# Attention and expert layer on one core: side products spread anew between the score blocks, and more masks laid by ScalarE

## What is computed

```python
# attention: 16 heads of 16; heads 0-3 see all earlier tokens, heads 4-15 a window of 64
qkv = xn @ w_qkv + b_qkv
w   = softmax(where(mask, -inf, q @ k.T * 16 ** -0.5))
att = concat_heads(w @ v) @ w_out + b_out
# experts: two branches (forward and inverse) of 8 experts of rank 64
prod    = (Q @ V) * cumsum(K @ W, axis=time)
weights = softmax(gelu(Q @ router_w1.T + b1) @ router_w2.T + b2 + bias)
branch  = (einsum(prod * weights, U) + weights @ b) / position
ffn     = (branch_fwd + alpha * branch_inv) @ W_O.T
```

## Time and profile before

| what | value |
|---|---|
| median of 3 runs | 1491.48 us (1486.11 to 1492.9) |
| the profiled execution | 1491.34 us, span 1489.6 us |
| busy TensorE, VectorE, ScalarE, GpSimd | 93%, 66%, 52%, 39% of the span |
| mean granted TensorE clock | 0.989 of full speed |
| DMA queue of SyncE | 150.59 MB, 38.8% of 16 engines' span |

### The profile page before, as it was taken

How to read it: one execution, slowest core, us unless ns; L and a number is a source line. 1 busy time by engine, 2 the same in 40 slices (tenths; PEclk the granted TensorE clock), 3 DMA queues, 4 the chain that set the end, 5 groups by cost and what they waited for, 6 DMA issues and landing times.

```text
span 1489.6 us, 35980 instructions
## 1 busy us (share of the span) xinstructions
PE 1379.5 (93%) x14481; PEld 1035.7 (70%) x14481; DVE 989.5 (66%) x2082; ACT 776.1 (52%) x1368; POOL 586.5 (39%) x663
## 2 busy tenths in 40 slices
PE   5978999999999999999999999999999999999996
PEld 4567685777758677586856778587775868667773
DVE  6667777567756777557875677566875578656661
ACT  2434537455464735645374554646356453755544
POOL 1025343453514444253433525144452534335341
PEclk9999999999999999999999999999999999999998
DMA  8430625326062541616353171624516153431610
GB/s 189 102 94 11 168 79 127 105 65 174 25 175 70 121 126 49 166 32 151 96 123 107 40 196 30 158 87 107 141 42 163 44 146 100 118 109 42 172 40 15
DMA packets 166614, 152.88 MB, mean 103 GB/s; under 512 B 37809, under 2 KB 149808, under 8 KB 166448
## 3 DMA queue, kind: packets, MB, share of 16 engines
q1 hardware_dynamic: 166448, 150.59, 38.8%
HBM read 108.57 MB, written 35.65 MB: 97 GB/s over the span
## 4 chain that ended last, share of the span: by engine, by line
PE 62%; DVE 15%; ACT 8%; issue 6%; DMA 4%; POOL 2%; SPq 1%; ACTq 0%; POOLq 0%; DVEq 0%
PE PS L676 30%; PE PS L787 11%; PE PS L821 4%; DVE rest L1193 3%; PE PS L880 3%; ACT HE L1063 3%; PE PS L807 3%; PE PS L909 3%; PE PS L898 2%; PE PS L963 2%; DMA weights_d<-weights_t 2%; DVE area L1198 2%; DVE area L1196 2%; ACT HE L1055 2%; ACT PS L1048 1%
## 5 line engine op out<-in xcount | busy, mean ns | idle before, releaser
L1504 POOL TENSOR_TENSOR PL<-prod,PH 128x512 fp32r<-128x512 f32 x128 | 164.7, 1287 | 201.3 <-ACT PH L1037 201.3
L676 PE MATMUL PS<-XH,WH 128*128 128x512 f32 x512 | 218.6, 427 | 21.7 <-ACT prod L1027 10.3
L1037 ACT ACTIVATE PH<-prod 128x512 fp32r<-128x512 f32 x128 | 80.8, 632 | 268.8 <-DVE prod L1305 252.8
L1499 POOL TENSOR_TENSOR prod<-prod,rest 128x512 f32<-128x512 f32 x96 | 124.8, 1303 | 242.9 <-DMA rest<-weights_d 166.6
L1229 DVE TENSOR_REDUCE block_peak<-PS 128x4 f32<-128x512 f32 x288 | 179.8, 685 | 48.0 <-PE PS L821 47.9
L676 PE MATMUL PS<-XH,WL 128*128 128x512 f32 x512 | 204.1, 399 | 0.0
L676 PE MATMUL PS<-XL,WH 128*128 128x512 f32 x512 | 203.6, 398 | 0.0
L1482 POOL TENSOR_SCALAR_AFFINE_SELECT HE<-HE 128x256 f32<-128x256 f32 x128 | 51.2, 406 | 364.2 <-ACT HE L1063 360.6
L1063 ACT ACTIVATE HE<-PS 128x512 f32<-128x512 f32 (+1 forms) x320 | 159.9, 553 | 33.5 <-PE PS L880 30.5
L1305 DVE TENSOR_TENSOR prod<-PS,prod 128x512 f32<-128x512 f32 x128 | 87.8, 686 | 97.3 <-PE PS L676 84.5
L676 PEld LDWEIGHTS PS<-XH,WH 128*128 128x128 f32 x512 | 97.1, 190 | 63.2 <-ACT prod L1027 16.8
(11 more groups left out here) (186 smaller groups left out, 3064.6 us busy)
## 6 DMA issues: line engine op xcount, KB each, us to landing
parts_d<-area SPq DMA_DIRECT2D x32, 768.0 KB, 5.0
area<-parts_d SPq DMA_DIRECT2D x128, 192.0 KB, 7.9
rest<-weights_d SPq DMA_DIRECT2D x192, 128.0 KB, 3.0
area<-parts_d SPq DMA_DIRECT2D x32, 576.0 KB, 7.8
tok<-in_L_attn_x_dram SPq DMA_DIRECT2D x16, 512.0 KB, 6.2
xt<-in_L_attn_x_dram SPq DMA_DIRECT2D x16, 512.0 KB, 4.1
wide<-weights_d SPq DMA_DIRECT2D x64, 128.0 KB, 3.0
out_dram<-xt SPq DMA_DIRECT2D x16, 512.0 KB, 3.8
```

Of the source, the lines that this page charges most:

```text
L676: ins = e.matmul(ps, a, b, start=first and k == 0, stop=last and k == n - 1, skip_group_check=True)
L1037: e.activation(PH[:, h, :], prod[:, j % 3, :], ACT.Copy).then_inc(phi)
L1499: e.tensor_tensor(prod[:, j % 3, :], prod[:, j % 3, :], wide[j % WIDE], ALU.mult).then_inc(weighed)
L1504: e.tensor_tensor(PL[:, j % 2, :], prod[:, j % 3, :], PH[:, j % 2, :].bitcast(F32), ALU.subtract).then_inc(plo)
```

## The change

1. The first three lpeak masks of each chunk but the first, and that of lscore (1, 0, 1), are laid by ScalarE. The three lpeak masks stand in the global stage, before its last gav; the fourth lpeak, on bank 4, keeps TensorE's mask. The peaks' banks start anew at bank 5 in each chunk.
2. x(1) and x(2) of the next chunk move from behind the global stage into it; values(1) moves from there to behind the last gav, and values(0), now on bank 7, to just before the last gav. vshift and the global stacks follow values(1). gate_parts stands one group earlier, finish(ch, 0) in the middle. weigh(0), (1) and (2) stand together behind chigh.
3. The last two groups of the expert stage, c(7) with product(7) and mix(6), stand behind all peaks.
4. In the local stage both turns stand behind the first unit; mix(7), both sums and the rows behind the second; and one parts block behind each of the others.
5. The last gscore tile is computed in all its 256 columns a head rather than 128; what is read of it is as before.
6. In the first chunk norm(1) runs in one piece behind the first four peaks, x(1) comes before it and x(2) after it. In the last chunk finish(15, 0) stands in the middle of the global stage instead of behind its first score pair.

```diff
--- before.py
+++ after.py
@@ -180,7 +180,7 @@
             add("parts_out", ch, w)
 
     def add_values(ch, u):
-        add_on("values", ch, u, uses=["bank2" if ch else f"bank{2 + u}"])
+        add_on("values", ch, u, uses=[("bank7", "bank2")[u] if ch else f"bank{2 + u}"])
         if u == T // 2 - 1:
             add("vshift", ch)
 
@@ -243,7 +243,7 @@
                 order[-1].append((add_seed, scores[2 * n + 3][4], "lscore", *scores[2 * n + 3][:4]))
             if n:
                 order[-1].append((add_lav, ch, *units[n - 1]))
-        return order
+        return order, [(add_seed, scores[1][4], "lscore", *scores[1][:4])]
 
     def global_groups(ch):
         order = []
@@ -258,7 +258,7 @@
 
         order = []
         for j in range(2 * KB):
-            if j < 2 * KB - 1 and (j > 1 or not ch):
+            if 1 < j < 2 * KB - 1:
                 order.append([(add_x, ch, j + 1, part) for part in range(2)] + [(add_weigh, ch, j + 1)])
             order.append([(add_c, ch, j, part) for part in range(2)] if j else [])
             order[-1].append((add_product, ch, j))
@@ -308,11 +308,12 @@
 
     def peak_groups(ch):
         c = ch % NC
+        turns["peak"] = 0
         order = [[(add_lpeak, ch, t, grp, peak_use())] for t in range(T) for grp in range(NL // 4)]
         gpeaks = [[(add_gpeak, ch, t, j, peak_use())] for t in range(T) for j in range(c * T + t + 1)]
         masks = [[] for _ in order + gpeaks]
         for n, ((stage, *key),) in enumerate(order + gpeaks):
-            if stage is add_lpeak and n >= PEAKS:
+            if stage is add_lpeak and (n >= PEAKS or ch and n < PEAKS - 1):
                 masks[n].append((add_seed, key[-1], "lpeak", *key[:-1]))
             elif stage is add_gpeak and key[2] == c * T + key[1]:
                 masks[n].append((add_seed, key[-1], "gpeak", *key[:-1]))
@@ -320,11 +321,9 @@
         gpeaks[2].append((add_rows, ch, 0))
         gpeaks[-1].append((add, "found", ch, 1))
         order += gpeaks
-        if ch == 0:
-            add_norm(1, order)
         blocks = range(0, len(order), PEAKS)
         joined = lambda groups, n: [stage for group in groups[n:n + PEAKS] for stage in group]
-        return [joined(order, n) + joined(masks, n + PEAKS) for n in blocks]
+        return [joined(order, n) + joined(masks, n + PEAKS) for n in blocks], joined(masks, 0)
 
 
     add("boot")
@@ -379,30 +378,44 @@
     add_weigh(0, 0)
     for part in range(2):
         add_c(0, 0, part)
+    for part in range(2):
+        add_x(0, 1, part)
+    add_weigh(0, 1)
 
     for ch in range(CHUNKS):
         nxt = ch + 1 < CHUNKS
 
-        experts, peaks = expert_groups(ch), peak_groups(ch)
+        experts = expert_groups(ch)
+        peaks = next_peaks if ch else peak_groups(ch)[0]
         split = len(experts) - (0 if nxt else 4)
         if ch:
             experts[1].append((add_finish, ch - 1, 1))
-            experts[2], experts[3] = experts[3], experts[2]
-        run(experts[0] + peaks[0])
-        weave(experts[1:split], peaks[1:])
+        experts[2], experts[3] = experts[3], experts[2]
+        if ch:
+            run(experts[0] + peaks[0])
+        else:
+            run(peaks[0])
+            for n in range(len(NORM)):
+                add("norm", 1, n)
+            run([(add_x, 0, 2, part) for part in range(2)] + [(add_weigh, 0, 2)] + experts[0])
+        weave(experts[1:split - 2], peaks[1:])
+        locals_, first_mask = local_groups(ch)
+        for group in [first_mask] + experts[split - 2:split]:
+            run(group)
         if ch:
             add_residual(ch)
 
         last_mix = [(add_mix, ch, 2 * KB - 1, part) for part in range(2)]
         if nxt:
-            side = [[(add_turn, ch + 1, 0)], last_mix, [(add_turn, ch + 1, 1)], [(add, "sums", ch + 1, 0), (add_rows, ch, 1)]]
-            side += [[(add_parts, ch + 1, 1, 0), (add, "sums", ch + 1, 1)]]
-            side += [[(add_parts, ch + 1, w, b)] for w, b in ((1, 1), (0, 0), (0, 1))]
+            side = [[(add_turn, ch + 1, 0), (add_turn, ch + 1, 1)]]
+            side += [last_mix + [(add, "sums", ch + 1, 0), (add, "sums", ch + 1, 1), (add_rows, ch, 1)]]
+            side += [[(add_parts, ch + 1, w, b)] for w in (1, 0) for b in range(DB)]
             if ch + 2 < CHUNKS:
                 side[-1].append((add, "load", ch + 2))
         else:
-            side = [[(add_rows, ch, 1)]] + experts[split:] + [last_mix]
-        weave(local_groups(ch), side)
+            side = experts[split:] + [last_mix]
+            side[0] = side[0] + [(add_rows, ch, 1)]
+        weave(locals_, side)
         add_lav(ch, NL // 4, 1)
         add("cturn", ch, 0)
         if not nxt:
@@ -414,33 +427,36 @@
                 add_hidden(ch + 1, j)
 
         order = global_groups(ch)
-        side = []
         if nxt:
-            first_x, first_c = ([(add, ch + 1, 0, part) for part in range(2)] for add in (add_x, add_c))
-            run(first_x + order[0] + first_c)
+            x0, x1, x2 = ([(add_x, ch + 1, j, part) for part in range(2)] for j in range(3))
+            run(x0 + order[0] + [(add_c, ch + 1, 0, part) for part in range(2)])
             add("logits", ch + 1, uses=["bank7"])
             add("chigh", ch, 0)
+            if ch + 2 < CHUNKS:
+                add_norm(ch + 2, order[1:])
+            steps = 2 + 3 * (ch % NC)
+            last = len(order) // 2 - 1
+
+            order[1] += [(add_gates, ch + 1), (add, "crest", ch, 0)]
+            for n, other in ((0, [(add_gate_parts, ch + 1)]), (steps // 2, x1), (steps, x2), (steps + steps // 2, [(add_finish, ch, 0)]),
+                             (last - 1, [(add_values, ch + 1, 0)])):
+                order[2 * n + 2] += other
+            next_peaks, first_masks = peak_groups(ch + 1)
+            order[2 * last] += first_masks
             order = order[1:]
-            if ch + 2 < CHUNKS:
-                add_norm(ch + 2, order)
-            side = [[(add_gates, ch + 1)], [(add_gate_parts, ch + 1)]] + [[]] * (2 * (ch % NC))
-            side += [[(add_values, ch + 1, 0)], [(add_values, ch + 1, 1)]]
-            side[0].append((add, "crest", ch, 0))
         else:
             add("crest", ch, 0)
-        side.append([(add_finish, ch, 0)])
-        weave(order, side)
+            order[len(order) // 2].append((add_finish, ch, 0))
+        for group in order:
+            run(group)
         if nxt:
+            add_values(ch + 1, 1)
             add("stacks", ch + 1, "global")
-        if nxt:
-            add_weigh(ch + 1, 0)
-            run([(add_x, ch + 1, 1, part) for part in range(2)])
-            add_weigh(ch + 1, 1)
         add("cturn", ch, 1)
         add("chigh", ch, 1)
         if nxt:
-            run([(add_x, ch + 1, 2, part) for part in range(2)])
-            add_weigh(ch + 1, 2)
+            for j in range(WIDE):
+                add_weigh(ch + 1, j)
         add("crest", ch, 1)
     add_finish(CHUNKS - 1, 1)
 
@@ -717,7 +733,7 @@
                             wh, wl = WH[:, k, COL_V:COL_V + D], WL[:, k, COL_V:COL_V + D]
                             xh, xl = XH[:, k, t * P:(t + 1) * P], XL[:, k, t * P:(t + 1) * P]
                             pairs += [(xh, wh), (xh, wl), (xl, wh)]
-                        ins = mms(psum(i, lo=a * D, hi=(a + 1) * D), pairs)
+                        ins = mms(psum(i, lo=a * D, hi=(a + 1) * D), pairs, first=a == 0)
                     ins.then_inc(values_ps)
 
                 elif kind == "hidden":
@@ -872,7 +888,7 @@
                     ch, j, half, pair = key
                     c = ch % NC
                     i, _ = where[stage]
-                    lo = max(0, (j - c * T) * P - half * HALF)
+                    lo = max(0, (j - c * T) * P - half * HALF) if (j, half) != tiles(c)[-1] else 0
                     q.wait_ge(peak_in[1], 16 * (ch + 1))
                     take(i, *stage)
                     for a in range(2):
```

## The result

The changed kernel takes 1537.49 us (median, 1530.1 to 1540.97) against 1488.8 us for the kernel before in the same comparison: a ratio of 1.0319, 95% interval 1.0278 to 1.0359. The forecast was 1502 with a range to 1514. The direction came true; the loss of 48.7 us between the medians is some four times the 11 us that I had forecast. The profiled execution of the changed kernel took 1540.97 us, with a span of 1539.3, which is 49.7 us more than before.

The account below looks back on a forecast made before the run. The prediction took TensorE, busy for 93% of the span, as the bound where it had no other wait. Terms +4.8 - 7 + 0 + 3 - 4.5 = -4, clock +15: 1491.3 - 4 + 15 = 1502 us, range 1474 to 1514.

Parts of the forecast that it names:

- VectorE's row before product(0): Last gav to c(1): 5.6 us in even chunks, 4.7 plus 0.3 in odd ones, c(1) waiting for it.
- Masks off TensorE: Three lpeak masks and one lscore mask to ScalarE: 1.2 us a chunk, 18 us over 15 chunks at most.
- Even windows: First global score to c(1), eight chunks: 20.7 us against 20.1, +4.8 in all; TensorE stands about 2.5 us.
- Odd windows: First global score to c(1), seven chunks: 30.3 us against 31.28, -7 in all; TensorE stands about 1.7 us.
- Gap before lav(2,0): Local stage: TensorE waits 2.3 us for GpSimd's select behind both sums; stage -0.4 odd, +0.3 even, 0 in all.
- Expert stage: Last two groups behind all peaks: product(7) 1.2 us earlier in odd chunks; no term of its own in the sum.
- First chunk: norm(1) in one piece before product(0): c(1) of chunk 0 starts 2.7 us later, +3 with a clock fall.
- Last chunk: finish(0) in the middle waits for nothing: -3.2 us and 1.5 for the clock, -4.5 in all.
- The clock: Of 23 gaps of 2.3 to 2.5 us half fall to 1.2 GHz, 1.5 us each: +15, bounds 0 and 35.
- Rival 1: Gaps come at TensorE but its clock does not fall: 1487 us (1481 to 1494), chance 0.27.
- Rival 2: Gaps are covered by tighter VectorE and GpSimd rows, masks give 18 us: 1472 us (1465 to 1484), chance 0.19.
- Rival 3: Global stacks land late for gpeaks in odd chunks' experts, eight times 1.4 us on top: 1513 us, chance 0.09.

Follow-up runs that it names:

- masks-alone kernel: The kernel before with only the four masks a chunk laid by ScalarE, all other order as before: 1496.87 us, ratio 1.0067.
- kernel with both edits back and the last chunk mended: Changed kernel with x(1), x(2) and local side work at old places, last chunk's chigh(0) and crest(0) behind the sixth global group: 1476.24 us, 0.9914.
- filler kernel: Changed kernel plus eight extra matmuls of 512 columns, never read, before c(1) of every chunk but the first: 1519.83 us, ratio 1.0214.

## Why the prediction was right in direction and wrong in size

Both gaps stand where the prediction put them, with the causes that it gave. Five terms of the sum were wrong. Without the clock it came to about +22 us instead of -4, and the clock to about +27 instead of +15, of the 49.7 us between the profiled executions. The steps that failed are VectorE's row before product(0), which was given almost nothing for the weighs of GpSimd beside it; the regrouping of the experts, whose price was left out; the local stage, taken as even; the last chunk, where the next wait was not looked for; and the clock, for which the gaps at odd boundaries were not counted.

- **Masks off TensorE**: right. One per chunk is left, and they gave about what they cost where TensorE had no other wait: 1.09 us in the odd windows of the masks-alone kernel, for three masks priced at 0.96.
- **Even windows, forecast 20.7, measured 21.56** (+11.7 instead of +4.8). The last gav ended 14.95 us after the first score (forecast 14.8). The step that failed is VectorE's row, taken at 5.9 us with 0.2 of it for the weighs: from the last gav to c(1) the mean was 6.6. In the one window without a meeting it was 5.65, as forecast; with three meetings it was 8.2. (The shortest, 5.4, is that of the last even boundary, which met one weigh but had no tokens to scale.) I had named the three weighs beside the row and priced them at nearly nothing.
- **Odd windows, forecast 30.3, measured 31.02** (-1.8 instead of -7). The last gav ended at 25.72 instead of 25.3, so the moved blocks filled less than I thought, and the row took 5.3 instead of 5.0: ctok meets the last weigh. The row of 4.7 us that I read before the change already held 0.46 us of a meeting (crest at 623.19, 1.16 us); with none it is 4.35, as the kernel with the weighs held back shows. With x(1) and x(2) back the window is 30.24, the length that I had forecast, but that is chance: it is about what the masks alone give (30.19), and not the path of the forecast.
- **Gap before lav(2,0), forecast 2.3 us, measured 2.12 and 1.77**: right, with its cause. What was wrong is the sum of the local stage, taken as 0. The even local stages came out 0.7 us longer than before where the clock held (26.06 against 25.34), the odd ones 0.3 shorter (26.01 against 26.28); forecast were +0.3 and -0.4. Without falls that is some 4 us in all instead of 0.
- **Expert stage**: forecast nothing. Regrouping costs 0.57 us in each, 8 us in all. My forecast took its benefit in the local stage and left out its price here.
- **First chunk, forecast +3**: c(1) starts 5 us later (100.03 against the earlier trace rows) behind a gap of 9.07 us, yet the first local score came at 134.55 against 134.66. In the seven kernels with the same work ahead of it as the changed one this point lay between 131.6 and 134.7, and in the two with the old order at 131.7 and 134.66, so the price stays open.
- **Last chunk, forecast -4.5, measured -0.2**, and that small sum is chance. In the global stage, for which the gain was forecast, the chunk lost 0.9 us: the wait for finish(0) went, and TensorE stood 2.96 us at the next thing in ScalarE's queue. The expert stage lost 1.4, behind the fall at 1452, and the local stage, in which the clock had fallen before, gained 2.4. With the wait moved too the global stage gains 3.5 us against before, and the whole stretch 5.3.
- **The clock, forecast +15, measured about +27**. Of 23 gaps I let half fall, by the two gaps of 1.94 and 1.95 us, of which one fell. Of those 23 there fell 11, but this is luck: all eight at even boundaries and three of the 15 before lav(2,0). The step that failed is what was left out. The seven odd gaps, forecast at 1.7 us and not counted, were 2.21 us long, by the meeting of ctok with a weigh, and all seven fell; with that meeting gone they were 1.27 and none did. Fourteen of the 15 falls at boundaries have an expert stage behind them, 7 x 1.94 + 7 x 1.55 = 24.4; three local falls at some 1.5 make 29, and the one of before at the earlier trace rows goes off: 27. A rate for all gaps alike, taken from two of them, did not hold for either kind.

The rule of the Trainium skill (TensorE: Matmul & The Clock Gate, section "Why this matters for your kernels"), which warns of longer gaps than those forecast, would have given -4. Six of the eight even gaps did come out longer than I had forecast, 3.19 to 5.14 us, and fell as it says. But the runs also go against it: gaps of 2.21 us brought the lower clock seven times of seven.

Rival 1 (the clock holds) fell with that. Rival 2 (the masks come through, as the gaps are covered) fell in this kernel. The kernel with both edits back and the last chunk mended comes near its time (1476.24 us against 1472), but by putting the cover back, which is not what that rival said. Rival 3 (global stacks late) did not show: the expert stages behind even boundaries are 38.31 us with the clock held, that is the 37.7 of before and 0.6 for regrouping.

## What to carry to other kernels

Before moving filler away from where it stands, ask which other engine's row it covers. Here x(1), x(2) and three masks covered five microseconds of VectorE in front of product(0). Once they were gone TensorE stood for 2 to 5 us, and the clock charged up to 2 us more behind it, in a stage where nothing waited; adding useless matmuls into the gap made the kernel some 16 us faster. Work taken off an engine just in front of such a wait gives nothing back, and a queue mended at one wait has to be walked on to the next.

## What the runs showed of the hardware

- A fall of TensorE's clock cost 1.2 to 1.55 us when it lasted 3.4 us, and 2.1 where it lasted 6.8, part of which lay in the gap itself.
- Falls are not decided by the gap alone. Gaps of 1.27 us never fell and those of 2.21 at boundaries always did. But one of 2.44 us at a boundary held in the filler kernel, and before the change the clock fell at 1438.9, in the last local stage, where no gap was longer than 0.9 us. The gap before lav(2,0), with the same blocks around it and 2.12 us long in even chunks (1.75 to 1.79 in odd ones), held at 688.93 in the changed kernel and fell at 674.62 with x back: 3 of 15 there and 12 of 15 here, 12 with the weighs held back, 8 with the filler. The three kernels where the clock held at some or all boundaries fell more often in the local stage. What decides it these runs do not tell; a price for one gap can't be carried to another kernel that way.
- VectorE was held up by 0.46 to 1.0 us per meeting with a weigh, the less the later it started beside it, and a weigh that started beside a held crest took 1.72 us instead of 1.27 (at 182.33). In one even window the four token scalings met two weighs and took 3.37 us instead of 1.38, and crest took 1.28 instead of 0.70: that was the longest gap, 5.14 us.
